# A graph-attention kernel: the score work of a group moved from its middle to its end, on three engines

## The reference

```python
def _gat_layer(x, src, dst, W, b, a, g, beta, N, concat):
    h = x @ W.T + b
    s_src = h @ a[:d]
    s_dst = h @ a[d:]
    score = s_src[src] + s_dst[dst]
    e = jnp.exp(-jax.nn.leaky_relu(score, ALPHA))
    h_prime = jax.ops.segment_sum(e[:, None] * h[dst], src, num_segments=N)
    ...
heads = [_gat_layer(embeds, src, dst, ..., concat=True) for i in range(8)]   # 64 wide each
out = _gat_layer(concatenate(heads), src, dst, ..., concat=False)            # 256 wide
```

## Time and profile before

| | us |
|---|---|
| median of three runs (6851.06 to 6879.34) | 6864.75 |
| the profiled execution | 6873.33 |
| its span, from the first to the last instruction | 6871.5 |
| TensorE busy in the span | 5194.1 (76%) |
| VectorE busy | 4274.9 (62%) |
| GpSimd busy | 3275.6 (48%) |
| ScalarE busy | 2400.3 (35%) |
| mean share of the TensorE clock that was granted | 0.887 |

### The profile page before, as it was taken

One profiled execution on the slowest core, in us unless ns is written; L12 is line 12 of the kernel. 1 busy time (PEld: TensorE's weight loads), 2 busy tenths in 40 slices (PEclk: granted clock), 3 DMA queues, 4 the chain that ended last, 5 costly groups with the idle time before them and its releaser, 6 DMA issues. The chain is left out here.

```text
span 6871.5 us, 96747 instructions
## 1 busy us (share of the span) xinstructions
PE 5194.1 (76%) x21312; PEld 2884.9 (42%) x21312; DVE 4274.9 (62%) x15762; ACT 2400.3 (35%) x6496; POOL 3275.6 (48%) x3459
## 2 busy tenths in 40 slices
PE   4577888867777777777777775787777777787787
PEld 2322222233333333333333333565655655565565
DVE  4688999966667667766676763444444444444443
ACT  2005777722333333333333332233333333333333
POOL 0000000016666666666666664666666666666662
PEclk8789999988989999989999996888888888888888
DMA  2100000016666666766676675444444444444444
GB/s 82 46 1 0 0 0 0 0 34 197 201 196 202 196 199 198 206 198 199 200 202 197 198 190 132 114 114 115 118 114 117 113 115 112 116 114 112 116 115 54
DMA packets 325650, 847.59 MB, mean 123 GB/s; under 512 B 73909, under 2 KB 97661, under 8 KB 325256
## 3 DMA queue, kind: packets, MB, share of 16 engines
q0 software_dynamic: 224256, 690.38, 37.1%
q1 hardware_dynamic: 101000, 152.57, 7.5%
HBM read 816.28 MB, written 26.36 MB: 123 GB/s over the span
## 5 line engine op out<-in xcount | busy, mean ns | idle before, releaser
L988 POOL DMA_INDIRECT out_rows<-table,shared_node_of x1712 | 1634.4, 955 | 1007.2 <-issue 461.7
L988 POOL DMA_INDIRECT heads_rows<-table,shared_node_of x1712 | 1620.1, 946 | 1017.5 <-issue 461.8
L1174 PE MATMUL heads_banks<-heads_rows,heads_hot 128*128 128x512 f32 x3424 | 1844.9, 667 | 249.1 <-DVE heads_rows L1045 142.3
L1174 PE MATMUL out_banks<-out_rows,out_hot 128*128 128x256 f32 x3424 | 1272.9, 464 | 326.7 <-DVE out_hot L1049 173.8
L1045 DVE TENSOR_TENSOR heads_rows<-heads_rows,heads_ps_k 128x512 f32<-128x512 f32 x1712 | 1160.9, 678 | 1.0
L1121 ACT ACTIVATE sums<-heads_banks x856 | 510.1, 600 | 1790.0 <-PE heads_banks L1174 985.6
L1174 PEld LDWEIGHTS heads_banks<-heads_rows,heads_hot 128*128 128x128 f32 x3424 | 622.6, 205 | 792.3 <-issue 660.8
L1121 ACT ACTIVATE late_sums<-out_banks x856 | 326.0, 383 | 1780.7 <-PE out_banks L1174 1033.5
L1174 PEld LDWEIGHTS out_banks<-out_rows,out_hot 128*128 128x128 f32 x3424 | 671.9, 221 | 525.8 <-issue 382.1
L853 PE MATMUL sort_ps_a<-sort_by_tile,sort_by_lane 125*128 125x367 f16 x1650 | 542.1, 330 | 148.1 <-ACT sort_by_lane L766 83.6
L647 DVE TENSOR_SCALAR sort_by_tile<-sort_count_tiles_h,sort_src_i 125x367 f16<-125x367 f16 x1650 | 613.5, 379 | 0.3 <-issue 0.2
(11 more groups left out here) (345 smaller groups left out, 6690.1 us busy)
## 6 DMA issues: line engine op xcount, KB each, us to landing
heads_lanes<-lane_rows SPq DMA_DIRECT2D x214, 256.0 KB
out_lanes<-lane_rows SPq DMA_DIRECT2D x214, 256.0 KB
heads_rows<-table,shared_node_of POOLq DMA_INDIRECT x1712
out_rows<-table,shared_node_of POOLq DMA_INDIRECT x1712
table<-proj_rows SPq DMA_DIRECT2D x50, 253.9 KB
table<-mid_rows SPq DMA_DIRECT2D x50, 127.0 KB
proj_x_raw<-in_x POOLq DMA_DIRECT2D x5, 1250.0 KB, 15.7
moe_x_raw<-in_x SPq DMA_DIRECT2D x50, 125.0 KB
```

What stands on the lines that cost most here:

```text
L988: nc.gpsimd.indirect_dma_start(out=rows[:, g % RING, j, :], out_offset=None, in_=table[:, :], in_offset=bass.IndirectOffsetOnAxis(ap=node_ ...
L1174: ins = nc.tensor.matmul(banks[:, bass.ds(info[r], width)], hot[:, g % HOTS, j, :], rows[:, g % RING, j, 0:width], start=False, stop=True, ...
```

## The change

Four calls are moved within a group; nothing is added or taken away.

- VectorE: `reduce_pieces(g+2)` from before weigh 0 to behind weigh 3; `add_target(g+2)` from behind weigh 0 to behind `make_hot`; `make_leaky(g+2)` from behind weigh 1 to the group's end, behind the woven-in work of step 3.
- ScalarE: the exponential of g+2 from behind the group's first copy to behind its second.
- TensorE: the scores of g+3 from behind the group's second step to behind its fourth.

```diff
@@ VectorE, for g in range(GROUPS)
                     nc.vector.tensor_copy(near[:, g % 2, :, :], weight[:, g % 3, :, :]).then_inc(s["brought"], 1)
-                if g + AHEAD < GROUPS:
-                    reduce_pieces(g + AHEAD)
                 if by_row:
                     dve.wait_ge(s["brought"], base["brought"] + g + 1)
                 weigh(g, 0)
-                if g + AHEAD < GROUPS:
-                    add_target(g + AHEAD)
                 extra.upto(g * GROUP)
                 weigh(g, 1)
-                if g + AHEAD < GROUPS:
-                    make_leaky(g + AHEAD)
                 extra.upto(g * GROUP + 1)
                 weigh(g, 2)
                 if g + TURN_AHEAD < GROUPS:
                     make_turn(g + TURN_AHEAD)
                 extra.upto(g * GROUP + 2)
                 weigh(g, 3)
+                if g + AHEAD < GROUPS:
+                    reduce_pieces(g + AHEAD)
                 if by_row and g + AHEAD < GROUPS:
                     make_hot(g + AHEAD)
+                if g + AHEAD < GROUPS:
+                    add_target(g + AHEAD)
                 extra.upto(g * GROUP + 3)
+                if g + AHEAD < GROUPS:
+                    make_leaky(g + AHEAD)
@@ ScalarE
-                    if j == 1 and g + AHEAD < GROUPS:
+                    if j == GROUP - 1 and g + AHEAD < GROUPS:
                         make_weight(g + AHEAD)
@@ TensorE
-                    if j == 1 and ahead:
+                    if j == GROUP - 1 and ahead:
                         source_scores(g + SCORE_AHEAD, block_ids(info[2 * PER:]))
```

## The result

The changed kernel takes **6953.7 us** in the median of four runs (6933.7 to 6960.6), the kernel before 6859.8 on the same chip: a ratio of **1.0127, 95% interval 1.0105 to 1.0149**. I had forecast 6776 us, and the time lies 4 us above the range.

What follows compares the result with a forecast made beforehand. The prediction took the loop between TensorE, VectorE and ScalarE, with late signals, to bound the kernel. Its terms, -246 + 98 + 59 = -89 us, led from a median of 6864.75 to 6776 us, range 6650 to 6950.

Steps and rivals of the forecast that it cites:

- Reduction off the front of the group: On VectorE, weigh 0, 1 and 2 no longer stand behind the wait for the scores: 246 us gained.
- The same signal, one step later: On VectorE, a late scores signal now stops the turning ahead of weigh 3: 98 us, 40% of the gain, come back.
- the rival in which nothing moves: TensorE's idle time only moves from the sums to the bank openings, GpSimd's ring setting the delay: 6865 us, chance 0.19.
- theory C: Late signals come only when the gathers have run out, so any order waits for them somewhere; idle time only changes place.
- VectorE's boundary: Small steps in a row between weigh 3 and the next weigh 0 cost 59 us, 35 of them in the heads layer.
- Scores at the end of the group: On TensorE, the four score products cost nothing by being moved behind the fourth step: 0 us.
- The exponential: On ScalarE, the exponential behind the second copy is still early enough for its group: no change, 0 us.
- The slower rival: Late scores stop the turning and weigh 3, and TensorE's reduction and scores precede the table load: 6969 us, chance 0.25.

Runs made afterwards that it cites:

- leaky_late_2: The change with the heads layer's leaky step moved behind the next group's weight copy: 6006.5 us, 1.0009 of the kernel before, on a chip of 6002 us.

## Why the prediction was wrong

**Reduction off the front of the group, -246.** Sound in its place, and near in size: in front of step 0, 178 us are gone in the output layer (163 forecast for the layer) and 29 in the heads layer (83 forecast). I had taken a third of the heads layer's idle time as the reduction's, which was too much.

**The same signal, one step later, +98.** Right in its place, too small, and not the whole of what comes back. In front of step 3, behind the turning that waits 358.1 us, 129 us are new in the heads layer and 25 in the output layer, 154 in all. Together with the first term this leaves the sums' idle time 63 us lower, where the forecast had 146. The openings add 38 (129 more in the output layer, behind a copy whose signal is late, 91 fewer in the heads layer). That is how the rival in which nothing moves had it (theory C), as far as TensorE's idle time goes. I gave it 0.19.

**VectorE's boundary, +59.** In the heads layer the pairs cost 98 us of VectorE's time, not 35, since I priced only the waits that could be seen and took the order behind them as free; I had not seen that the reduction had covered the copy's result for weigh 0. On the chips of 6000 us this time counts: without the two pairs 40 of the 45 us are gone. On a chip of 6920 us putting the pairs together costs nothing. On the first chip, too, VectorE is idle 803 us of the heads layer before (2616 - 1813), so I suppose that the term's true value there is about 0; it wasn't measured there.

**Scores at the end of the group, 0.** This is a step that failed. Moving the scores alone costs 0.7% on a chip of 6000 us and 1.7%, 108 us, on a chip of 6921, more than the whole result, both in an order that has the reduction behind weigh 1. I had named what stands behind the scores in TensorE's queue and then left it out, because TensorE would seldom be the late one. What the pairs show in its place is a late score that stops VectorE wherever its next reader stands (the reduction's wait of 138.1 us becomes 604.4), and a TensorE that is busy longer. Whether TensorE's row at the boundary costs anything by itself stays open: `leaky_late_2` has it and stands at 1.0009.

**The exponential, 0.** Right: 0.9994.

**No term at all: TensorE's busy time.** This is the other step that failed, and in the account of the first chip it is the larger. With -25 us of idle time by the groups' rows the sum should have come out a little below before. The 83 us by which TensorE was busy longer, at a granted clock of 0.90 and 0.84 in place of 0.91 and 0.86, made it +60. My sum took TensorE's busy time as fixed.

**The slower rival** gave 6969 us, near the result. One half of its mechanism shows in the heads layer: the late `scored` stops the turning, and step 3 comes late. The other half, TensorE's row, doesn't: its mark was that the openings' idle time without a copy as its cause rises by 100 us or more, and it fell, from 150.1 to 100.5 and from 163.2 to 156.9. That its number is near is partly luck, and its sum has a slip: it leaves 98 us of gain where the first two terms leave 148, and with 148 it gives 6919 us.

## What to carry to other kernels

Idle time that an order takes away in front of one instruction has to be looked for in front of the next ones of the same engine, and the sum needs a line for the engine's busy time: here it rose by 83 us, at a lower granted clock, while the idle time fell by 25. Small steps spread between large independent ones are cheap by their place: on VectorE a pair of dependent neighbours costs 0.115 us here, and it cost the kernel something on a chip of 6000 us and nothing on one of 6920. Work moved later on TensorE makes its signal later by as many steps: before taking it as free, find what reads that signal next, and what stands behind this reader.

## What the runs showed of the hardware

**The same kernel takes 6000 us on some chips and 6860 to 6921 on others.** Of six chips three are of each kind. The clearest difference between the traces is in the late signals. The reduction's wait in the output layer of the kernel before, 805.2 us and mostly "remote" in the earlier trace rows, is on chip 7:

```profile
L1027 DVE TENSOR_REDUCE out_score<-out_ps_s 128x4 f32<-128x12 f32 x425 | 72.8, 171 | 249.9 <-PE out_ps_s L1144 247.4
```

No "remote" is left. On the first chip, 190 of the heads layer's 856 copies start at a signal that comes over 0.3 us after the modelled end of the run's last product, 3.3 us on average and up to 10.1; on chip 7 there are none in that layer. Of these 190, 63% come within 0.06 us of a gather's signal and 74% when GpSimd has been idle for over 0.3 us; of the layer's other timed signals it is 46% and 33%. I had them as a property of the kernel. They are one of the chip, or of the occasion, since no numbered chip was used on two occasions; what delays them there stays open.

**Long idle stretches of TensorE and its lower clock go together.** In the output layer of the kernel before, on the first chip, 26 of 31 idle stretches of over 3 us were followed by a sums' matmul at the lower level, and 17 of 129 of those of 0.5 to 1 us. The change raised the number of the long ones from 31 to 43 there, with 126 and 168 us, though the idle time as a whole changed little. In the heads layer their number and time hardly changed (39 with 174 us, 43 with 175), but 30 of them now stand directly in front of a sums' matmul, where 4 had. The Trainium skill (TensorE: Matmul & The Clock Gate, HAM oscillation — how this bites in real kernels) has idle gaps between bursts of matmuls send the clock back to its lower level each time, and the trace agrees in so far as most of the long stretches are followed by the lower level. That this is the whole of the 83 us is not shown.
